# B products of four items turned on TensorE, step size summed in PSUM, three more C products on GpSimd, in a recurrent decoder stage

## The reference, cut to what matters

```python
def _selective_scan(u, dt, A, Bm, Cm, Dp):
    dA = jnp.exp(dt[..., None] * A)
    dBu = (dt * u)[..., None] * Bm[:, :, None, :]
    def step(h, inp):
        dA_t, dBu_t, C_t = inp
        h = dA_t * h + dBu_t
        y = jnp.einsum('ben,bn->be', h, C_t)
        return (h, y)
    ...
    return y + u * Dp

def _mamba(x, in_w, cw, cb, xw, dtw, dtb, A_log, Dp, ow):
    u, z = jnp.split(x @ in_w, 2, axis=-1)
    ...                                      # causal convolution of 4 taps
    u = jax.nn.silu(conv)
    dbl = u @ xw
    dt = jax.nn.softplus(dbl[..., :DT_RANK] @ dtw + dtb)
    Bm = dbl[..., DT_RANK:DT_RANK + D_STATE]
    Cm = dbl[..., DT_RANK + D_STATE:]
    A = -jnp.exp(A_log)
    y = _selective_scan(u, dt, A, Bm, Cm, Dp)
    return (y * jax.nn.silu(z)) @ ow
```

## Time and profile before

| | us |
|---|---|
| median of 3 runs | 1765.83 |
| lowest, highest | 1758.49, 1766.81 |
| profiled execution | 1767.52 |
| its span, first to last instruction | 1765.8 |
| recurrent stage, first scan to end of last C product | 504.3 to 1349.4 |

### The profile page before, as it was taken

How to read it: one execution, slowest core, us unless ns; L and a number is a source line. 1 busy time by engine, 2 the same in 40 slices (tenths; PEclk the granted TensorE clock), 3 DMA queues, 4 the chain that set the end, 5 groups by cost and what they waited for, 6 DMA issues and landing times. The chain is left out here.

```text
span 1765.8 us, 23296 instructions
## 1 busy us (share of the span) xinstructions
...
## 2 busy tenths in 40 slices
...
DMA packets 70215, 168.03 MB, mean 95 GB/s; under 512 B 20420, under 2 KB 40152, under 8 KB 56664
## 3 DMA queue, kind: packets, MB, share of 16 engines
...
q0 software_dynamic: 256, 0.01, 0.0%
...
## 5 line engine op out<-in xcount | busy, mean ns | idle before, releaser
L1633 POOL TENSOR_TENSOR ma_hs<-ma_dtuR,ma_Bt 128x1024 f32<-128x1024 f32 x256 | 596.6, 2358 | 7.0 <-DMA ma_dtuR<-ma_dtu_d 6.7
L1816 ACT ACTIVATE ps<-ma_dtR,ma_A 128x512 f32<-128x512 f32 x512 | 332.7, 682 | 297.2 <-DVE ma_hs L1961 254.8
L845 POOL TENSOR_TENSOR x_pr<-x_pr,x_rec 128x512 f32<-128x512 f32 x256 | 267.4, 1045 | 291.6 <-DVE x_rec L1085 291.6
L1955 DVE TENSOR_TENSOR_SCAN ps<-ps,ma_hs 128x1024 f32<-128x1024 f32 x176 | 401.5, 2281 | 0.2
L1710 PE MATMUL ps<-ma_hs,ma_fold 128*32 128x512 f32 x1024 | 174.7, 816 | 206.1 <-POOL ma_hs L1641 177.4
L1051 ACT ACTIVATE x_pr<-x_sm,x_mx 128x256 f32<-128x256 f32 x512 | 255.2, 500 | 68.9 <-DVE x_mx L1076 65.9
L1961 DVE TENSOR_TENSOR ma_hs<-ps,ma_Ct 128x1024 f32<-128x1024 f32 x176 | 215.4, 1224 | 6.1
L1955 DVE TENSOR_TENSOR_SCAN ma_hs<-ps,ma_hs 128x1024 f32<-128x1024 f32 x80 | 182.5, 2281 | 18.3 <-ACT ps L1816 15.4
L1641 POOL TENSOR_TENSOR ma_hs<-ma_hs,ma_Ct 128x1024 f32<-128x1024 f32 x80 | 188.2, 2353 | 12.3 <-DVE ma_hs L1955 12.1
L1677 PE MATMUL ps<-ma_hn,ma_w_tap 128*128 128x512 f32 (+3 forms) x256 | 142.0, 707 | 52.4 <-ACT ma_hn L1840 52.4
L907 PE MATMUL ps<-ident,x_pr 128*128 128x128 f32 x1024 | 163.2, 286 | 5.4 <-DVE x_pT L985 4.4
...
## 6 DMA issues: line engine op xcount, KB each, us to landing
...
```

What stands on the lines that cost most here:

```text
L845: pool.tensor_tensor(pr[:, r, :, :], pr[:, r, :, :], rec[:, r, :].unsqueeze(2).broadcast_to([P, 2, L]), ALU.mult).then_inc(pr_done, 1)
L1633: pool.tensor_tensor(hs[:, k % SLOTS, :, :], dtuR[:, unit(f, h), q, :].unsqueeze(1).broadcast_to([P, 2, CH]), rows(Bt, k), ALU.mult).then_ ...
L1816: e = act.activation(c.ps[:, 2 * (k % 2) + a, :], dtR[:, unit(f, h), q, :], ACT.Exp, scale=A[:, (f // QUARTERS) % 2, h, q, no:no + 1])
L1955: dve.tensor_tensor_scan(out, pair(k), slot(k), 0.0, ALU.mult, ALU.add).then_inc(scan_done, 1)
```

## The change

The numbers of the items below are again t within a round.

1. **B products of items 12 to 15** (`TURNED`) are no longer POOL's. PE transposes dt*u of half 1 and B of the round (`turn_dtu`, `turn_b`), ACT copies both out of PSUM (`copy_dtu`, `copy_b`), and then makes 32 scaled copies of 128 x 128 a round (`scale_rows`: one [128,128] tile of dt*u times one column of B each, into `rowB`), in groups spread over t = 0 to 11 (`SCALED`). PE turns these back, eight transposes of 128 x 128 for each of the four items (`turn_rows`), into the PSUM pair of the item. The decays of these items go to the `hs` slot instead of PSUM; the scan takes its two inputs the other way round.
2. **The step**: the dt projection's weights are halved once a block (`half_steps`, ACT), so that PSUM holds x/2. PE adds |x|/2 to it by an identity matmul (`add_to_dt`), and later ln(1 + exp(-|x|)) in the same way. ACT copies dt out of PSUM (`step_size`, now at its t = 9), leaving out the first step of each sequence, whose large number is written once at the start. dt*u is DVE's now, out of PSUM, after `gate(f, 0)` of item 9.
3. **C products**: POOL has items 0, 4, 7, 9, 10, 12, 13 and 14; DVE the other eight.
4. `dtR` and `dtuR` have two buffers each, one for each half, and SP's order of stores and spreads follows. ACT's `square` moves from t = 10 to t = 11.
5. Outside the stage: the semaphores of the opening and of the first cross attention are given back one norm earlier, so that the stage can have more of them.

The diff, cut to its core:

```diff
-    NORM_D = set(range(16)) - {0, 4, 6, 10, 14}
+    NORM_D = set(range(16)) - {0, 4, 7, 9, 10, 12, 13, 14}
+    TURNED = {12, 13, 14, 15}
+    SCALED = {0: 4, 1: 4, 4: 4, 5: 2, 6: 2, 7: 2, 8: 4, 9: 4, 10: 3, 11: 3}
...
             @block.gpsimd
-                        if k + AHEAD < NK:
+                        if k + AHEAD < NK and not by_tensor(k + AHEAD):
                             times_b(k + AHEAD)
                         if not on_vector(k):
                             times_c(k)
-                        if t == 8 and f + 1 < NF:
-                            dt_times_u(f + 1)
...
             @block.tensor
+                def add_to_dt(F, ready, added, stop):
+                    pe.wait_ge(ready, F + 1)
+                    for h, bank in ((0, PA), (1, PB)):
+                        mm = pe.matmul(c.ps[:, bank, :], c.ident[:, :], dtu[:, h, :], start=False, stop=stop,
+                                       skip_group_check=True)
+                    mm.then_inc(added, 1)
...
+                def turn_rows(k):
+                    f, h, np_, q = place(k)
+                    pe.wait_ge(rows_done, 32 * (f + 1))
+                    if on_vector(k - 2):
+                        pe.wait_ge(c_vector, n_vector(k - 2) + 1)
+                    else:
+                        pe.wait_ge(scan_done, k - 1)
+                    for a in range(2):
+                        for t in range(4):
+                            mm = pe.transpose(c.ps[:, 2 * (k % 2) + a, t * P:(t + 1) * P],
+                                              rowB[:, t, a, q, :, :].rearrange("p e n -> p (e n)"), c.ident[:, :])
+                    mm.then_inc(turned, 1)
...
                         kv_job(4 * f + 1, Y[1])
+                    if F < NF:
+                        add_to_dt(F, abs_done, abs_added, False)
+                        add_to_dt(F, ln_done, ln_added, True)
+                    if 0 <= f < NF:
                         sum_y(f, 1)
...
                     if F < NF:
                         pe.wait_ge(dt_done, 2 * F + 2)
+                        pe.wait_ge(dtu_done, 2 * F + 2)
                     if G < NF:
                         centre(G)
...
             @block.scalar
+                def scale_rows(f, i):
...
+                    t, a, ni = i // 8, i // 4 % 2, i % 4
+                    act.activation(rowB[:, t, a, :, :, ni], dtuT[:, t, :].rearrange("p (e q) -> p q e", q=GQ), ACT.Copy,
+                                   scale=BT[:, t, a, ni:ni + 1]).then_inc(rows_done, 1)
...
                         if t == 11 and f >= 1:
                             residual(f - 1)
...
+                        if F < NF and t == 13:
+                            copy_b(F)
+                        if F < NF and t == 15:
+                            copy_dtu(F)
+                        for _ in range(SCALED.get(t, 0)):
+                            scale_rows(f, made)
+                            made += 1
...
             @block.vector
-                        if t == 8 and F < NF:
-                            step_size(F)
                         if t == 9:
                             gate(f, 0)
+                        if t == 9 and F < NF:
+                            dt_times_u(F)
```

More of the change, by code:

```diff
@@ L176, in _ @@
                     prefetch(sp)
+            if cleared:
                 @block.gpsimd
```

179 lines of the change are left out of this document (132 added, 47 removed).

## The result

| | before | after |
|---|---|---|
| median, us | 1763.94 (4 runs) | 1809.70 (4 runs) |
| lowest, highest | 1758.49, 1766.81 | 1807.04, 1813.25 |
| ratio after / before, 95% interval | | 1.0258, 1.0230 to 1.0286 |
| span of the profiled execution | 1765.8 | 1808.5 |
| first scan of the stage | 504.3 | 507.5 |

What follows compares the result with a forecast made beforehand. A loop of waits through POOL's 17 instructions was taken to set rounds of 52.8 us. Stage +13, start +4, end -2, plus 2 for tap projection and silus gave 1784.5 on the profiled run, 1783 against the median; range 1762 to 1824.

Steps and rivals of the forecast that it cites:

- Loads: Busy time per recurrent round after the change: DVE 48.2, POOL 46.8, ACT 44.4 us.
- the scaled copy: ACT's 32 copies a round: 0.26 us apart, 8.3 in all; far bound 0.5 for a strided write.
- ACT's last three copies: Scaled copies following `residual`: no bound at 0.26 each, as `average` ends later; 0.6 late at 0.5 each.
- The GpSimd loop: POOL's 17 instructions from C of item 12 to C of item 7, sum, gate, turn: 52.8 us a round; chance 0.60.
- the term of the sum: `sum_y(f, 1)` on PE within the loop: 2.8 us, half way between 1.92 fast and 3.64 slow.
- The check that the loop is the longest: From item 12 to the gate: DVE's own way 41.2 us against 44.5 by POOL; ACT's rows no bound.
- 2 for the tap projection and the silus: Allowance of 2 us added to the total because these now follow more PE work.
- rival C: ACT the bound at 0.5 us a scaled copy: ACT busy 52, rounds about 55, 1816 us; chance 0.07.
- The weights: Weight preparation on POOL stands in the loop in full: 5.2 us a block, 15.6 over three blocks.
- The start: Start of the recurrent stage, from the logarithm to the first spread: 4 us longer, 2.5 to 5.5.
- Rival A: The loop does not close and DVE sets the round: 49.6 us a round, 1726 us in all; chance 0.13.
- Rival B: PE at its low clock in turning items 12 to 15: round 55.9 us, 1824 in all; chance 0.20.

Runs made afterwards that it cites:

- e1: Changed kernel with its scaled copies written in four layouts, strided or contiguous on the read and write sides, values not the reference's; 1805.7 us, one run.
- e8: Changed kernel with only 8 of 32 scaled copies made and the second kv matmul run four times between the two additions to dt; 1784.1 us.
- e3: Changed kernel with PE's second tap projection moved ahead of the sum of batch 3; 1807.9 us, ratio 1.0238 to the kernel before.
- e9: Changed kernel with the C product of item 6 instead of item 7 on POOL; 1808.9 us, ratio 1.0257 to the kernel before.
- e11: Changed kernel with ordered copy reads, earlier second tap projection, kv matmul four times between the additions, and item 6, not 7, on POOL; 1755.7 us.
- e12: Changed kernel with ordered copy reads, earlier second tap projection, and item 6 instead of item 7 on POOL; 1757.1 us, ratio 0.9963 to the kernel before.
- e15: Changed kernel with POOL's C products put back to items 0, 4, 6, 10 and 14; 1797.1 us, ratio 1.0194 to the kernel before.

## Why the prediction was right and wrong

**Direction and stage**: right, but the loop that sets the round is another one (below). The rounds did not shrink to DVE's 48.2, because new waits close a loop at about their old length.

**Loads**: DVE 48.29 for 48.2, POOL 46.55 for 46.8. ACT came to 48.28 for 44.4. The term that failed is the scaled copy, taken at 0.26 "since size and scaling are the same" as in the pair of the earlier trace rows: the reads of that pair are in order, these are strided. It is 0.42, inside the bounds, nearer to the far one; 32 x 0.16 = 5 us of ACT; its other additions came 1.2 below their estimate. No row had shown the far bound of 0.5 "for a strided write"; in e1 it is the strided read that costs, and the strided write adds nothing to the distance. ACT's last three copies, called no bound at 0.26, end 0.3 late and hold up the turn of item 12 in every round.

**The GpSimd loop**: right as far as it went. 17 products took 39.5; POOL stood 8.1 a round (6 forecast), at items 9, 10 and 12 and nowhere between 12 and 7; the turn of item 12 cost DVE 1.2 and those of 13 to 15 nothing; the gates waited 3.0 a round for the sums, but that agreement is luck: the 3 was forecast for the gate of item 9 alone, which waited 1.61, and the other 1.37 are at the gate ahead of item 2. In e8 the loop is 52.4, for 51.9. With a slow sum it is 54.4 in e3 for 53.7: the term of the sum, "2.8, half way", was too low wherever the addition is done early, as PE idles then. In the changed kernel the sum took 2.65, near the 2.8, but for another reason: it ran directly behind the slow second addition.

**The check that the loop is the longest**: this step failed. It followed DVE's own way only, and for ACT looked at the last three copies and at "2 for the tap projection and the silus". The way from the C product of item 14 over sum, tap projection, silus, copies and logarithm to the same sum of batch 1 was not added up. It is 54.6, 1.8 above the forecast of 52.8. So the wait was wrong: the forecast had the second addition end some 1.7 us ahead of the sum, and the sum wait for POOL's C product of item 7; measured, the sum starts 1.3 after that product, when the addition ends. e9 shows that it is not POOL's product that is waited for: 2.3 us earlier, it changed nothing. The rival C named its cause, dearer copies and ACT's waits, with 55 a round and 1816, but asked for an ACT that is busy for over 50; a list with waits in it need not be full to set the round. Its 0.07 was too little.

**The sum**: 15 x 1.8 = 27 too low for the round. The weights were put at 5.2 a block on top of two ordinary rounds; they cost 112.7 - 2 x 54.6 = 3.5, since the round after is shorter, which gives 5 back. 27 - 5 = 22, near the stage's miss of 34.2 - 13 = 21. The start came out at +3.3, for +4. Behind the stage the -2 for the end is not to be seen in 417.9 for 412.6: kernels that have the same code there took between 410.5 (e15) and 420.3 (e9), so the +5.3 is within the spread between executions, and no run shows it to be an effect of the change. Together the miss is 42.7 - 17 = 26: 21 in the stage, 7 behind it, less the 2 set aside for tap projection and silus.

**Rival A**, the loop not closing, did not occur; e11 and e12 show rounds near it, 50.1 to 51.8, once both loops are shortened. **Rival B** did not occur either. The granted clock in the turning items (PE from 1214.85, and the second addition from 1255.41):

```profile
1214.85:1222.30 7.45, 7.45 (x58) 4.89 (x58) 6.32 (x4) 5.44 (x11) 3.95 (x2) 1.00 0.76 315
1255.41:1259.12 3.71, 3.71 (x4) 1.18 (x4) 3.68 (x3) 3.71 (x9) 3.71 (x3) 0.50 0.19 71
1259.12:1261.70 2.58, 2.58 (x17) 0.52 (x16) 1.13 (x1) 2.58 (x7) 2.42 (x2) 0.71 0.00 0
```

It is 1.00, the 2.4 GHz level, through 32 transposes and what stands between them, and 0.50, the 1.2 GHz level, in the second addition, behind 4.24 us in which PE was idle; it rises again in the course of the sum. The Trainium skill says, in TensorE: Matmul & The Clock Gate, part on the PE-mode transpose, that the clock does not count transposes as activity. The trace does not bear out what the prediction feared from it: sixteen transposes took 1.97 and eight 1.09, each with a matmul group between them. No run here has transposes alone for long.
